# Graph attention kernel: rows ordered by oct, 64-column attribute tiles, weighted sums ahead of the transposes, and a gather that leaves out rows without an edge

## The reference

```
e     = (edge_attr @ We.T).reshape(-1, HEADS, C)
k_e   = k[src] + e
v_e   = v[src] + e
alpha = sum(q[dst] * k_e, axis=-1) / sqrt(C)
amax  = segment_max(alpha, dst)            # over the edges of each destination
ex    = exp(alpha - amax[dst])
denom = segment_sum(ex, dst)
out   = segment_sum(v_e * (ex / denom[dst])[..., None], dst)
```

## Time and profile before

| | before |
|---|---|
| median of 3 runs | 4986.42 us |
| profiled execution, its own time | 4956.95 us |
| profiled execution, span from first to last instruction | 4954.7 us |
| TensorE matmul busy | 3986.7 us (80%) |
| VectorE busy | 1796.9 us (36%) |
| ScalarE busy | 1483.9 us (30%) |
| GpSimd busy | 1938.6 us (39%) |
| gathers (queue 0) | 159520 packets, 523.41 MB, 34.7% of 16 engines' span |
| other DMAs (queue 1) | 478740 packets, 141.70 MB, 13.9% |
| granted TensorE clock, mean | 0.845 |

### The profile page before, as it was taken

The page is one execution under the profiler, slowest core; times in us unless marked ns, Lnnn a source line. Parts: engine busy times, 40 slices in busy tenths (PEclk is TensorE's granted clock), DMA queues, the critical chain, the costliest instruction groups (busy, mean ns, idle before and its releaser), DMA issues. The chain is left out here.

```text
span 4954.7 us, 86461 instructions
## 1 busy us (share of the span) xinstructions
PE 3986.7 (80%) x28082; PEld 2157.7 (44%) x28082; DVE 1796.9 (36%) x4770; ACT 1483.9 (30%) x3644; POOL 1938.6 (39%) x2075
## 2 busy tenths in 40 slices
PE   6787888888888888888888888888867778778778
PEld 3344444444444444444444444444434445445445
DVE  5233333333333333333333333333335454544553
ACT  2133232222232233232332323223223323323322
POOL 2255555555555555555555555555530000000000
PEclk9788888888898888888889898888888778868877
DMA  5566666666666666666666666666660000000000
GB/s 191 161 180 179 172 172 172 175 170 169 181 179 172 168 176 170 173 174 173 173 171 182 178 183 179 172 171 177 170 165 18 15 15 15 15 15 15 15 15 7
DMA packets 638315, 665.65 MB, mean 134 GB/s; under 512 B 408275, under 2 KB 501908, under 8 KB 638244
## 3 DMA queue, kind: packets, MB, share of 16 engines
q0 software_dynamic: 159520, 523.41, 34.7%
q1 hardware_dynamic: 478740, 141.70, 13.9%
HBM read 632.59 MB, written 33.05 MB: 134 GB/s over the span
## 5 line engine op out<-in xcount | busy, mean ns | idle before, releaser
L597 POOL DMA_INDIRECT F<-kv_rows,srci x1970 | 1894.3, 962 | 1622.8 <-PE pZ L860 970.7
L760 ACT ACTIVATE FT<-ring 128x512 f32<-128x512 f32 (+1 forms) x1182 | 581.8, 526 | 1890.4 <-PE ring L828 1005.9
L828 PE MATMUL ring<-ident,F 128*128 128x128 f32 x3940 | 752.2, 309 | 407.8 <-ACT FT L760 392.5
L860 PE MATMUL pZ<-F,PT 128*32 128x192 f32 x9408 | 793.2, 362 | 117.6 <-issue 114.2
L828 PEld LDWEIGHTS ring<-ident,F 128*128 128x128 f32 x3940 | 447.1, 151 | 859.0 <-ACT FT L760 565.7
L656 DVE TENSOR_REDUCE nmx<-pS 128x1 f32<-128x384 f32 x393 | 219.3, 558 | 1263.3 <-remote 1098.9
L662 DVE COPY PT<-pPT 128x384 f32<-128x384 f32 x393 | 219.2, 558 | 956.6 <-issue 522.9
L860 PEld LDWEIGHTS pZ<-F,PT 128*32 128x32 f32 x9408 | 263.2, 116 | 483.0 <-issue 442.2
L1106 POOL DMA_DIRECT2D out_dram<-accb x6 | 5.8, 960 | 1077.8 <-DVEq L1271 1077.8
L841 PE MATMUL pS<-FT,qh 128*32 128x320 f32 x3144 | 382.6, 567 | 17.9 <-issue 14.2
L844 PE MATMUL pS<-F,G 80*32 80x320 f32 x3144 | 386.5, 571 | 0.0
(11 more groups left out here) (200 smaller groups left out, 4427.7 us busy)
## 6 DMA issues: line engine op xcount, KB each, us to landing
F<-in_edge_attrT SPq DMA_DIRECT2D x788, 80.0 KB
F<-kv_rows,srci POOLq DMA_INDIRECT x1970
F<-in_dst SPq DMA_DIRECT2D x788, 20.0 KB
srci<-src_front SPq DMA_DIRECT2D x796, 1.5 KB
kv_rows<-kvs SPq DMA_DIRECT2D x7, 1792.0 KB, 6.4
qb<-q_cols SPq DMA_DIRECT2D x100, 64.0 KB
U<-in_x SPq DMA_DIRECT2D x7, 896.0 KB, 10.9
xn_rows<-xs SPq DMA_DIRECT2D x7, 896.0 KB, 6.3
```

Of the source, the lines that this page charges most:

```text
L597: pool.indirect_dma_start(out=F[s][:, t, 0:KV], out_offset=None, in_=kv_d, in_offset=bass.IndirectOffsetOnAxis(ap=srci[j % GB][:, col:col ...
L760: act.activation(FT[j % 2][:, :, t0 * P:t1 * P], ring[n % 2][:, 0:KD * w].rearrange("p (k e) -> p k e", e=w), ACT.Copy).then_inc(ring_empt ...
L828: m = pe.transpose(ring[n % 2][:, k * w + (t - t0) * P:k * w + (t - t0 + 1) * P], F[j][:, t, k * 3 * BLK:k * 3 * BLK + P], ident[:, :])
L860: m = pe.matmul(pZ[rows, 0:ZW].rearrange("p (x d) -> p x d", d=BLK), PT[:, t, rows], f, start=(t == 0), stop=(t == KB - 1))
```

## The change

It has four parts.

1. The rows of scores, weights and sums are ordered by oct first: row `o * HP + c * C + ...`. The selectors, masks and copies that know the order follow. Gathered rows are plain k then v (`D` = 256 each).
2. The attribute matmuls cover both halves of the heads of an oct at once: 64 stationary columns instead of 32. In `scores` the four attribute matmuls of 320 columns become two. In `z_part` four matmuls of 192 columns become four of 128 columns (values) and two of 64 columns (attributes).
3. The runs are not interleaved: `z_part` 0, 1 and 2 come first and raise `slot_free`, then the wait for the gathered slot, then `ft` 0, 1 and 2. ScalarE takes `weights`, then the copy to `Zs`, then the three `ft_out`.
4. VectorE computes gather indices `srcg` from `srci`: at positions behind the oct's last edge, the index becomes 65536 or more. The gather has `bounds_check=NP - 1, oob_is_err=False`, and leaves those rows out, so that a slot keeps there what it held. So that it holds finite numbers, all four slots are cleared once at the start of stage 2, and GpSimd waits for that.

```diff
@@ stage 1
+                sp.dma_start(brow[:, :], bound_d[0:NO + 1].partition_broadcast(P)).then_inc(bounds_landed, 16)
...
-                dve.wait_ge(bounds_landed, 16)
+                dve.wait_ge(bounds_landed, 32)
...
+                ch.step(dve.tensor_copy(browf[:, :], brow[:, :]))
+                ch.step(dve.tensor_sub(lenb[:, 0:NO], browf[:, 1:NO + 1], browf[:, 0:NO]))
+                ch.step(dve.tensor_scalar(lenb[:, 0:NO], lenb[:, 0:NO], SKIP, None, ALU.mult))
@@ gather
                             in_offset=bass.IndirectOffsetOnAxis(ap=srcg[j % GB][:, col:col + 1], axis=0),
+                            bounds_check=NP - 1, oob_is_err=False,
                         ).then_inc(gathered[s], 16)
+                pool.wait_ge(blank, 10)
@@ vector, start of stage 2 and join_indices
+                for s in range(SLOTS):
+                    dve.memset(F[s][:, :, 0:KV], 0.0).then_inc(blank, 1)
...
                     dve.wait_ge(idx_landed[j], value)
-                    dve.tensor_copy(srci[j][HP:P, KB - 1:KB], srci[j][HP:P, KB:KB + 1]).then_inc(idx_ready, 1)
+                    for o in range(2):
+                        w = slice(o * KB, (o + 1) * KB)
+                        dve.scalar_tensor_tensor(out=srcg[j][:, w], in0=posb[:, w], scalar=lenb[:, first(o)], in1=srci[j][:, w],
+                                                 op0=ALU.subtract, op1=ALU.max).then_inc(cut, 1)
+                    cuts[0] += 2
+                    dve.wait_ge(cut, cuts[1] + cuts[0])
+                    dve.tensor_copy(srcg[j][HP:P, KB - 1:KB], srcg[j][HP:P, KB:KB + 1]).then_inc(idx_ready, 1)
@@ scalar
+                            weights((j + 1) % GB, it * GB + (j + 2))
+                            act.wait_ge(slot_free, it * GB + (SLOTS + j + 1))
+                            act.activation(Zs[:, :], pZ[:, 0:ZW], ACT.Copy).then_inc(z_out, 1)
                             for q in range(len(PAIRS)):
                                 m = j * len(PAIRS) + q
                                 ft_out(j, q, RING0 + m, rb + (m + 1))
-                                if q == 0:
-                                    weights((j + 1) % GB, it * GB + (j + 2))
-                            act.wait_ge(slot_free, it * GB + (SLOTS + j + 1))
-                            act.activation(Zs[:, :], pZ[:, 0:ZW], ACT.Copy).then_inc(z_out, 1)
@@ tensor, scores
+                    for o in range(2):
+                        m = pe.matmul(pS[o * HP:(o + 1) * HP, o * HP:o * HP + OW],
+                                      G3[half][0:K3, g + o, :, :].rearrange("p c r -> p (c r)"),
+                                      F3[s][0:K3, o * OW:(o + 1) * OW], start=False, stop=True)
@@ tensor, z_part
-                            blocks = F[s][:, o * TO + t, :].rearrange("p (x d) -> p x d", d=BLK)
-                            f = blocks[:, 2:9:3, :] if c == 0 else blocks[:, 6:9, :]
-                            m = pe.matmul(pZ[rows, 0:ZW].rearrange("p (x d) -> p x d", d=BLK), PT[:, t, rows], f,
-                                          start=(t == 0), stop=(t == KB - 1))
+                            rows = slice(o * HP + c * C, o * HP + (c + 1) * C)
+                            pe.matmul(pZ[rows, 0:P], PT[:, t, rows], F[s][:, o * TO + t, D + c * P:D + (c + 1) * P],
+                                      start=(t == 0), stop=False)
+                    for o in range(2):
+                        rows = slice(o * HP, (o + 1) * HP)
+                        m = pe.matmul(pZ[rows, P:ZW], PT[:, t, rows], F[s][:, o * TO + t, KV:FP], start=False, stop=(t == KB - 1))
@@ tensor, step j
                             for t in range(KB):
                                 z = z_part(s, t)
-                                if t == KB - 1:
-                                    z.then_inc(slot_free, 1)
-                                if t == 0:
-                                    pe.wait_ge(gathered[s2], it * (16 * T * 2) + 16 * T * ((j + 2) // SLOTS + 1))
-                                pe.wait_ge(ring_emptied, rb + (m + t - 1))
-                                ft(s2, t, RING0 + m + t)
+                            z.then_inc(slot_free, 1)
+                            pe.wait_ge(gathered[s2], it * (16 * T * 2) + 16 * T * ((j + 2) // SLOTS + 1))
+                            for q in range(len(PAIRS)):
+                                pe.wait_ge(ring_emptied, rb + (m + q - 1))
+                                ft(s2, q, RING0 + m + q)
```

More of the change, by code:

```diff
@@ L140, in build @@
             nid = sbt(mid, "nid", [P, NG + 2])
-            G3 = [sbt(mid, f"G3{i}", [P, KD, HP // ON, C]) for i in range(2)]
+            G3 = [sbt(mid, f"G3{i}", [P, HP // ON, KD, C]) for i in range(2)]
             WeP = sbt(mid, "WeP", [P, HR, 2 * C])
+            lenb = sbt(mid, "lenb", [P, NO + 2 * GB])
+            posb = sbt(mid, "posb", [P, 2 * KB])
             sel_ready = sem("sel_ready")
@@ L296, in _ @@
                                 for h in range(HR):
[L297 to L299 removed]
+                                    for c in range(KD):
+                                        g3 = G3[i][:, :, c, :].rearrange("p (g o) r -> p g o r", o=2)[:, :, o, h * ON:(h + 1) * ON]
+                                        chp.step(pool.affine_select(out=g3, in_=g3, compare_op=ALU.not_equal, fill=-BIG,
+                                                                    base=-(DE + o * ON), pattern=[[0, HP // GN], [-1, ON]],
+                                                                    channel_multiplier=1))
+                        for o in range(2):
+                            chp.step(pool.iota(posb[:, o * KB:(o + 1) * KB], pattern=[[P, KB]], base=-o * HP, channel_multiplier=1,
+                                               allow_small_or_imprecise_dtypes=True))
+                        chp.step(pool.tensor_scalar(posb[:, :], posb[:, :], 0.5, SKIP, ALU.add, ALU.mult))
                         pool.sem_inc(sel_ready, 1)
@@ L462, in build @@
                 srci = [sbt(s2, f"srci{i}", [P, 2 * KB], I32) for i in range(GB)]
+                srcg = [sbt(s2, f"srcg{i}", [P, 2 * KB], I32) for i in range(GB)]
                 FT = [sbt(s2, f"FT{i}", [P, KD, CH]) for i in range(2)]
@@ L746, in _ @@
                             ch.step(dve.tensor_scalar(offs[:, NO:NO + 2 * GB], offs[:, 0:2 * GB], float(OW), float(E), ALU.add, ALU.min))
+                            ch.step(dve.tensor_scalar(lenb[:, 0:NO], lenb[:, 0:NO], -OW * SKIP, None, ALU.add))
+                            ch.step(dve.tensor_scalar(lenb[:, NO:NO + 2 * GB], lenb[:, 0:2 * GB], -OW * SKIP, None, ALU.add))
                             dve.sem_inc(pass_ready, 1)
```

84 lines of the change are left out of this document (40 added, 44 removed).

## The result

The changed kernel takes 5046.75 us (median of 4 runs, 5033 to 5053), the kernel before 4984.01 us beside it: a ratio of 1.0131, 95% interval 1.009 to 1.0171. It is slower by 1.3%, where the prediction said faster by 2%. The time lies within the range that was given, the direction was wrong. The profiled execution of the changed kernel took 5044.4 us with a span of 5042.8 us and a mean clock of 0.85.

The account below looks back on a forecast made before the run. Step time was taken as GpSimd's gather batch plus its wait for TensorE's sums. Terms -44 - 59 - 20 + 12 = -111 us gave 4846 us, 4875 as median; own range 4820 to 4960, whole range 4690 to 5110.

Parts of the forecast that it names:

- What bounds the kernel: Stage 2: GpSimd's batch of five gathers, 6.0 us, plus a 2.9 us wait for the sums makes the 8.9 us step.
- late notice: Stage 2: while gathers are issued, TensorE's results are noticed late; the loop closes 2.0 to 2.4 us after a batch's end.
- Sums first: TensorE in stage 2: earlier `slot_free` saves 44 us in steps 1 and 5 and 59 us in the six others.
- Work on TensorE: Three more tile-width switches, 0.24 to 0.45 us a step, hidden by the loop's 2.3 us wait; uncovered +137 us.
- Order on ScalarE: First key transposes wait for the exponential and the copy of the sums, 1.3 us and the copy; covered by the wait.
- Indices on VectorE: Two more operations ahead of the maximum, about 0.4 us a step, hidden by VectorE's idle time; uncovered +157 us.
- The gather: GpSimd's gather leaves out 17.8% of the rows and gets 10 ns shorter per instruction: -20 us.
- the bounds test costs: Rival: skipping rows makes each gather 0.1 us slower (0.06 to 0.16), +196 us, total 5091 us; chance 0.17.
- rival of a gather that goes by its rows: Gather instruction time falls with rows left out: -257 to -422 us in all, about 4650 us; chance 0.13.
- The start: Start of stage 2: clearing four slots and small operations delay the first gather, +12 us (8 to 16).
- TensorE becomes the bound: Rival: switches and ScalarE's order lengthen the chain between scores, 0.3 us a step comes through, 5096 us; chance 0.16.

Follow-up runs that it names:

- f1: The changed kernel, no edit, run again on a chip that doesn't hold TensorE: 1.0048 of the kernel before on that chip.
- e1: The changed kernel without the cut of rows (plain gather through uncut indices, no clearing of slots): 1.0103 of the kernel before.
- e4: The kernel before with only the sums first, in the new order on both TensorE and ScalarE: 4880 us, 0.9813 of the kernel before.
- e2: The kernel before with the cut of rows alone (indices, bounds in the gather, slots cleared at the start): 1.0027 of the kernel before.
- e16: The kernel before with sums first on TensorE alone and bounds in the gather, no row cut, on a chip that doesn't hold TensorE: 1.0035 of before.
- e9: The changed kernel without the cut, with mask and attribute matmuls in 32-column tiles, four in place of two each: 1.0123 of the kernel before.
- e7: The changed kernel without the cut, with all value matmuls of a step ahead of all its attribute matmuls: 4967 us, 0.9991 of the kernel before.
- e8: The kernel before with the sums first on TensorE alone, ScalarE's order as before: 4836 us, 0.9691 of the kernel before.
- e13: The changed kernel with VectorE's index operations moved from ahead of the maximum to last in its step: 1.0183 of the kernel before.
- e3: The changed kernel with bounds in the gather but uncut indices, so every row is fetched, and no clearing: 1.0044 of the kernel before.
- e19: The kernel before with sums first (TensorE and ScalarE) and a semaphore instruction behind each gather, on a chip that doesn't hold TensorE: 0.9781 of before.

## Why the prediction was wrong

**What bounds the kernel.** That step time is batch plus wait, and that the wait follows the batch's end by 1.0 us and something, is right for the late chips, and the trace of before was one. For the scores, late notice is right as well: VectorE's maximum starts 2.55 us after their modelled end in the changed kernel's trace (median) and 0.19 us after it in f1. Wrong was that the loop closes 2.0 to 2.4 us after the batch "whatever TensorE has done". The sums, for which the loop waits, are often not finished early: TensorE is held, and what is left of them comes behind the hold. So more work on TensorE lengthens the wait (e1 against e4), and a longer batch shortens it (e2).

**Sums first.** Forecast -103 us; e4 against before is -74 us by the two profiled spans (4880.3 and 4954.7) and 1.9%, 93 us, by ratio. The size is right and the make-up is not. Steps 1 and 5 gained 1.87 + 0.34 us of wait a block where I had 0.6 + 0.3. The six ordinary steps lost 0.1 us each where I had a gain of 0.2.

**Work on TensorE: the step that failed.** I had 0.24 to 0.45 us a step, put at nothing because "the 2.3 us in which the loop waits hides it", and an uncovered price of 137 us. It wasn't hidden: 147 us, or 0.37 us a step, reached the time (e1 against e4). The cover was the hold itself, which was no slack. The size was low too. The traces of f1 and e16 show 1.04 us a step at full clock, so that by this measure some two thirds were still covered. I had counted three changes of width more than in the interleaved order, at 0.08 us each at full clock, from one pair of starts. Against the sums-first order there are seven more (eight in place of one, from scores to key transposes), and one costs about 0.15 us (1.04 / 7). The split of one 192-column matmul into two, which I had at nothing, costs next to nothing in pace (1.19 us for e9's sums), but on a late chip the longer row of matmuls is held for longer (e9, as slow as e1). e7 puts four changes at 59 us there.

The rule I had cited from the Trainium skill, "TensorEngine Tiling (Array Packing)", Key Properties, that a change of tiling mode drains the array, did speak against the change, and e7 agrees with it: 0.15 us a step less with four changes fewer. I had set it beside a row that gave about half of its price, and then hidden that.

**Order on ScalarE.** "Hidden" is wrong both ways: it costs 1.3% on a late chip (e4 against e8) and saves the changed kernel 3.7% on a prompt one.

**Indices on VectorE.** Hidden, as forecast: e13 gained nothing by moving them.

**The gather.** I had -10 ns; it is +53 ns, by the test alone (e3), and leaving rows out saves no time. The rival "the bounds test costs" had the mechanism, and its price of 0.06 to 0.16 us an instruction was just too high. But its 196 us didn't arrive on the late chip (e2: 13 us with the start). They do arrive where GpSimd's loop is the bound (e16 against e19: 106 us). The rival of a gather that goes by its rows, beside which I had cited the Trainium skill, "DMA: Bandwidth & Descriptors", SWDGE vs HWDGE vs iDMA, is refuted: 18% of the data is gone and the instruction is no shorter.

**The start.** +12 forecast, +11.1 measured.

**The sum by its parts,** in stage 2, from the first gather to the last exponential: 3480 us before; -76 for the sums first (e4, 3404); +172 for rows and tiles (e1, 3576); -12 for the cut (3564). With 11 us at the start and -7 us behind stage 2 that is 88 us, the difference of the two spans (5042.8 - 4954.7). The profiled executions lie off their medians, before's by 27 us below and e1's by 23 us above; by medians and ratios the parts are -93, +146 and +14 us, the last with the start in it (67 in all, where the medians differ by 63). The rival "TensorE becomes the bound" (5096 us, 0.3 us a step coming through) is the one whose mechanism came closest, with 0.16 of the chances. That of the costly test gave nearly the same time, 5091 us, and on a late chip its mechanism didn't decide.

**Still open:** what holds TensorE while gathers are issued, why two chips don't do it, why bounds in the gather take 0.6% off on a late chip, why e8 beats e4, and how much of these differences goes through the clock.

## What to carry to other kernels

A wait that looks like slack is cover only if the engine that is waited for has finished: look at the gaps marked "issue" inside its own work before you hide anything behind it. When a matmul is split to save columns, count the changes of tile width in the whole step, and read their price from a stretch where the engine runs unhindered. And undo the parts of a change one by one: here the sums first, on TensorE alone, beat the kernel before by 3% and the changed one by 4% on the late chips (it wasn't run on a prompt one), and the rest of the change ate it.

## What the runs showed of the hardware

- While GpSimd issued indirect gathers, TensorE was held on two of the four chips of the experiments: the changed kernel's sums at full clock took 3.86 us (median) where more than half of them lay within a batch, and 1.93 where they lay outside. On another chip (f1) the same kernel's took 1.93 within a batch, and its wait before one was 0.36 us in place of 2.73. The kernel before took 18% less on such chips (4072 us against 4984).
- On a late chip VectorE took up the changed kernel's scores 2.55 us after their modelled end (median), on a prompt one 0.19 us after (f1).
- `bounds_check` adds 53 ns to an indirect gather of 128 rows (949 to 1002 ns), whether rows fall out or not; the count of packets stays, the bytes fall.
- Three parts of the sums take 1.16 us as 12 matmuls of 192 columns, and 1.94 us as 12 of 128 columns in 32-column tiles and 6 of 64 columns in 64-column tiles in turn (full clock). With the 6 behind the 12 they take 1.36 (e7), and as 24 matmuls in 32-column tiles 1.19 (e9), where nothing holds them.
- TensorE's clock was at its lower level for 16 to 38% of stage 2 on the late chips and for 0 to 4% on the prompt ones.
